# First layer: softmax in two halves, two score banks, output projection in four parts, POOL products in pieces of 512 elements

## What is computed

```python
x = x + tanh(g_xattn[0]) * xattn(layernorm(x), ctx, mask)   # 16 heads of 64, causal, then out @ Wo.T + bo
x = x + tanh(g_ffn[0])   * ffn(layernorm(x))
def ffn(x):
    h = rmsnorm(x) * gamma1
    q = h @ Wq + bq                                  # 16 heads of 16 per token
    k, v = split((h @ Wdown + bdown) @ Wup + bup)
    att = softmax(einsum('bthd,btgd->bthg', q, k) / 4)   # per token: 16 x 16 scores among its own heads
    x = x + einsum('bthg,btgd->bthd', att, v) @ Wo + bo
    h2 = rmsnorm(x) * gamma2
    gate = softmax(h2 @ Wg + bg)                     # 8 experts, all of them computed
    return x + sum_e gate_e * (h2 @ We_e)
```

## Time and profile before

| | |
|---|---|
| median of the runs | 2658.17 us |
| profiled execution, its own time / span | 2663.2 us / 2661.4 us |
| busy over the span | PE 87%, DVE 56%, ACT 48%, POOL 38% |
| granted TensorE clock over the span | 0.956 |
| one body of the loop in layer 0 | 78.4 us |

### The profile page before, as it was taken

One profiled execution on the slowest core, in us unless ns is written; L12 is line 12 of the kernel. 1 busy time (PEld: TensorE's weight loads), 2 busy tenths in 40 slices (PEclk: granted clock), 3 DMA queues, 4 the chain that ended last, 5 costly groups with the idle time before them and its releaser, 6 DMA issues. The chain is left out here.

```text
span 2661.4 us, 48220 instructions
## 1 busy us (share of the span) xinstructions
PE 2325.5 (87%) x16128; PEld 1931.7 (73%) x16128; DVE 1487.3 (56%) x3906; ACT 1268.0 (48%) x3971; POOL 1019.5 (38%) x910
## 2 busy tenths in 40 slices
PE   5888989888888898888466999999999999999998
PEld 4667777777777777776354777877777887777777
DVE  3467667666766676767635445444444544444441
ACT  5655566555556555556023444433344443334441
POOL 1355554555554455555512333222233322223320
PEclk9989999999999999999667999999999999999999
DMA  4000000000000000000040000000000000000000
GB/s 145 14 6 17 13 16 4 16 16 16 16 12 4 16 16 16 16 4 9 4 161 1 13 17 16 16 16 16 4 12 16 16 16 16 16 4 12 16 9 9
DMA packets 25856, 51.66 MB, mean 19 GB/s; under 512 B 6272, under 2 KB 7040, under 8 KB 24640
## 3 DMA queue, kind: packets, MB, share of 16 engines
q1 hardware_dynamic: 25792, 50.84, 5.7%
HBM read 42.44 MB, written 8.39 MB: 19 GB/s over the span
## 5 line engine op out<-in xcount | busy, mean ns | idle before, releaser
L1191 POOL TENSOR_SCALAR l_probs<-l_probs,l_rinv 128x256 f32<-128x256 f32 x512 | 238.4, 480 | 590.0 <-DVE l_rinv L1406 589.4
L1302 ACT ACTIVATE l_probs<-l_score,l_negmax 128x256 f32<-128x256 f32 x512 | 238.4, 472 | 265.0 <-DVE l_negmax L1401 265.0
L364 POOL TENSOR_TENSOR l_prod<-l_att,l_kv 128x2048 f32<-128x2048 f32 x64 | 287.4, 4527 | 180.7 <-DVE l_att L637 180.7
L350 POOL TENSOR_TENSOR l_prod<-l_q,l_kv 128x2048 f32<-128x2048 f32 x64 | 290.3, 4547 | 155.9 <-DVE l_att L620 84.1
L1606 PE MATMUL l_ffn<-l_w,l_hid 128*128 128x256 f32 x1536 | 347.9, 382 | 1.0 <-ACT l_hid L1276 1.0
L1606 PEld LDWEIGHTS l_ffn<-l_w,l_hid 128*128 128x128 f32 x1536 | 287.6, 190 | 51.0 <-issue 14.3
L1413 DVE COPY l_probsT<-l_attn 128x512 f32<-128x512 f32 x256 | 175.5, 685 | 161.1 <-PE l_attn L1569 160.9
L710 DVE CUSTOM_DVE_ANT_0 l_probs<-l_score,l_mbias 128x256 f32<-128x256 f32 (+1 forms) x512 | 161.3, 353 | 147.5 <-PE l_score L906 97.6
L1401 DVE TENSOR_REDUCE l_negmax<-l_score 128x2 f32<-128x512 f32 x256 | 175.1, 684 | 65.4 <-PE l_score L1557 65.4
L643 DVE TENSOR_REDUCE l_h<-l_prod 128x128 f32<-128x2048 f32 x64 | 146.3, 2286 | 110.7 <-POOL l_prod L364 110.7
L439 ACT ACTIVATE l_probs<-l_probs,l_negmax 128x256 f32<-128x256 f32 x256 | 130.8, 511 | 107.7 <-DVE l_negmax L710 106.5
(11 more groups left out here) (271 smaller groups left out, 7527.2 us busy)
## 6 DMA issues: line engine op xcount, KB each, us to landing
l_ctxin<-in_ctx SPq DMA_DIRECT2D x32, 256.0 KB, 3.0
l_xin<-in_x SPq DMA_DIRECT2D x16, 256.0 KB, 2.7
l_x<-in_x SPq DMA_DIRECT2D x16, 256.0 KB, 2.6
x<-l_acc SPq DMA_DIRECT2D x16, 256.0 KB, 2.0
l_xin<-x SPq DMA_DIRECT2D x16, 256.0 KB, 3.3
l_x<-x SPq DMA_DIRECT2D x16, 256.0 KB, 2.6
out<-l_x SPq DMA_DIRECT2D x16, 256.0 KB, 2.0
l_hid<-in_w SPq DMA_DIRECT2D x2, 1536.0 KB, 8.6
```

The source lines that it names most:

```text
L350: nc.gpsimd.tensor_tensor(prod[:, u].rearrange("p (h g d) -> p h g d", h=half, g=H), q4[:, u * half:(u + 1) * half].unsqueeze(2).to_broadc ...
L364: nc.gpsimd.tensor_tensor(prod[:, u].rearrange("p (h d g) -> p h d g", h=half, d=HD), a4.unsqueeze(2).to_broadcast([P, half, HD, H]), v4.u ...
L1191: last = nc.gpsimd.tensor_scalar(probs[:, j % 4, t * S:(t + 1) * S], probs[:, j % 4, t * S:(t + 1) * S], rinv[:, j, t:t + 1], 1.0, ALU.mul ...
L1302: last = nc.scalar.activation(probs[:, s % 4, t * S:(t + 1) * S], ps[:, t * S:(t + 1) * S], ACT.Exp, bias=negmax[:, s, t:t + 1], accum_out ...
```

## The change

What it does: `attn_out` takes two of eight chunks at a time, at steps 10, 14, 18 and after step 19, and adds them up in a bank of its own (`outer`); for that bank `score` goes from three to two. The mix steps move up and `down` comes before `q`. Scores, softmax and gather move up, the softmax is done per half of the tokens, and POOL's second products wait for their half alone. Each POOL product is written as four instructions of 512 elements per partition.

```diff
+PART = 2
-        attn = Banks(nc, ctx, "l0_attn", attn_uses + ["out"], ahead=["xT", "k0", "k1", "k2", "v0", "v2"])
-        mix_at = {2: "hT", 3: "q", 4: "down", 5: "up0", 6: "up1"}
+        outer = Banks(nc, ctx, "l0_outer", ["out"], 1)
+        attn = Banks(nc, ctx, "l0_attn", attn_uses + ["idle"], ahead=["xT", "k0", "k1", "k2", "v0", "v2"])
+        mix_at = {1: ("hT",), 2: ("down", "q"), 3: ("up0",), 4: ("up1",)}
-        score_at = {7: 0, 9: 1, 11: 2, 12: 3}
-        gather_at = {15: 0, 16: 1, 18: 2, 19: 3}
-        score = Banks(nc, ctx, "l0_score", [f"s{j}" for j in range(H)] + ["idle0", "idle1"], 3)
+        score_at = {6: 0, 7: 1, 9: 2, 10: 3}
+        soften_at, divide_at = {7: 0, 10: 1}, {8: 0, 11: 1}
+        gather_at = {11: 0, 13: 1, 14: 2, 16: 3}
+        score = Banks(nc, ctx, "l0_score", [f"s{j}" for j in range(H)])
         side = SideBanks(nc, ctx, "l0_side", mix_uses, moe_uses,
-                         ["oT", "out", "hT", "q", "down", "h2T", "up0", "gate", "up1"] + ...
+                         ["oT", "out", "hT", "down", "q", "up0", "up1", "h2T", "gate"] + ...
 query_key (POOL), and weigh (POOL) in the same way:
-                    nc.gpsimd.tensor_tensor(
-                        prod[:, u].rearrange("p (h g d) -> p h g d", h=half, g=H),
-                        q4[:, u * half:(u + 1) * half].unsqueeze(2).to_broadcast([P, half, H, HD]),
-                        k4.unsqueeze(1).to_broadcast([P, half, H, HD]), ALU.mult).then_inc(prod_ready, 1)
+                    for h in range(0, half, PART):
+                        last = nc.gpsimd.tensor_tensor(
+                            out[:, h:h + PART], q4[:, u * half + h:u * half + h + PART].unsqueeze(2).to_broadcast([P, PART, H, HD]),
+                            k4.unsqueeze(1).to_broadcast([P, PART, H, HD]), ALU.mult)
+                    last.then_inc(prod_ready, 1)
 weigh:
+                    if u == 0:
+                        pool.wait_ge(att_ready, 2 * b + t + 1)
                     if piece < 2:
-                        pool.wait_ge(att_ready, b + 1)
+                        pool.wait_ge(scored, 4 * b + piece + 3)
 beside_head (ACT), now after the projections' copies:
-                    if b is not None and s == 12:
-                        act.wait_ge(sub_ready, b + 1)
-                        nc.scalar.activation(att[:], att[:], ACT.Exp, scale=HD ** -0.5).then_inc(aexp_done, 1)
+                    if b is not None and s in soften_at:
+                        t = soften_at[s]
+                        act.wait_ge(sub_ready, 2 * b + t + 1)
+                        nc.scalar.activation(att[:, t], att[:, t], ACT.Exp, scale=HD ** -0.5).then_inc(aexp_done, 1)
 DVE: mix_softmax_max(b, t) and mix_softmax_divide(b, t) work on att[:, t]; a drain behind the divide is gone
+                        if s in soften_at:
+                            mix_softmax_max(b, soften_at[s])
+                        if s in divide_at:
+                            mix_softmax_divide(b, divide_at[s])
 PE:
+                def attn_out(a, j):
+                    ps, full, free, turn = outer.at("out", a)
+                    heads.emptied(pe, f"o{j}", a)
+                    if j == 0:
+                        ...
+                        pe.wait_ge(free, turn)
+                    for t in range(NT):
+                        for c in (2 * j, 2 * j + 1):
+                            last = T.matmul(ps[:, t * D:(t + 1) * D], oT[:, c, t * P:(t + 1) * P], wo[:, c, :],
+                                            start=t == 0 and c == 0, stop=t == NT - 1 and c == NC0 - 1)
+                    if j == 3:
+                        last.then_inc(full, 1)
+                            if s in (10, 14, 18):
+                                attn_out(a, (s - 10) // 4)
                     if a is not None:
-                        score.skip(pe, "idle0", a)
-                        score.skip(pe, "idle1", a)
+                        attn.skip(pe, "idle", a)
+                        attn_out(a, 3)
```

More of the change, by code:

```diff
@@ L363, in weigh @@
                     a4 = att[:, t].rearrange("p (h g) -> p h g", g=H)[:, u * half:(u + 1) * half]
-                    nc.gpsimd.tensor_tensor(prod[:, u].rearrange("p (h d g) -> p h d g", h=half, d=HD),
-                                            a4.unsqueeze(2).to_broadcast([P, half, HD, H]), v4.unsqueeze(1).to_broadcast([P, half, HD, H]),
-                                            ALU.mult).then_inc(prod_ready, 1)
+                    out = prod[:, u].rearrange("p (h d g) -> p h d g", h=half, d=HD)
+                    for h in range(0, half, PART):
+                        last = nc.gpsimd.tensor_tensor(out[:, h:h + PART], a4[:, h:h + PART].unsqueeze(2).to_broadcast([P, PART, HD, H]),
+                                                       v4.unsqueeze(1).to_broadcast([P, PART, HD, H]), ALU.mult)
+                    last.then_inc(prod_ready, 1)
                 def body(a, b, c, nxt):
@@ L470, in before_exp @@
                 def before_exp(b, c, s):
-                    if b is not None and mix_at.get(s) == "hT":
+                    if b is not None and "hT" in mix_at.get(s, ()):
                         high(side, "hT", b, hT[0], hT_hi, gamma1)
-                    if b is not None and mix_at.get(s) == "down":
+                    if b is not None and "down" in mix_at.get(s, ()):
                         ps, full, _, turn = side.at("down", b)
@@ L544, in _ @@
             def _(dve):
-                for banks in (attn, score, heads, side):
+                for banks in (attn, score, heads, outer, side):
                     banks.open(dve)
@@ L718, in attn_final @@
                 def attn_final(a):
-                    ps, full, free, turn = attn.at("out", a)
+                    ps, full, free, turn = outer.at("out", a)
                     dve.wait_ge(full, turn)
@@ L737, in beside_head @@
                             V.tensor_copy(x1res[:], x1[:]).then_inc(x1_copied, 1)
-                    if b is not None and s in mix_at:
-                        use = mix_at[s]
-                        if use == "hT":
-                            low(side, "hT", b, hT, hT_hi, gamma1)
-                        elif use == "q":
-                            mix_queries(b)
-                        elif use == "down":
-                            mix_down(b)
-                        else:
-                            mix_kv(b, int(use[2:]))
+                    if b is not None:
+                        for use in mix_at.get(s, ()):
+                            if use == "hT":
+                                low(side, "hT", b, hT, hT_hi, gamma1)
+                            elif use == "q":
+                                mix_queries(b)
+                            elif use == "down":
+                                mix_down(b)
+                            else:
+                                mix_kv(b, int(use[2:]))
                     if c is not None:
@@ L956, in beside_head @@
                 def beside_head(b, c, s):
-                    if b is not None and s in mix_at:
-                        use = mix_at[s]
-                        if use == "hT":
-                            pe.wait_ge(h_ready, b + 1)
-                            transpose4(side, "hT", b, h)
-                        elif use == "q":
-                            side.emptied(pe, "hT", b)
-                            tokens(side, "q", b, hT, fq, D)
-                        elif use == "down":
-                            mix_down(b)
-                        else:
-                            mix_up(b, int(use[2:]))
+                    if b is not None:
+                        for use in mix_at.get(s, ()):
+                            if use == "hT":
+                                pe.wait_ge(h_ready, b + 1)
+                                transpose4(side, "hT", b, h)
+                            elif use == "q":
+                                tokens(side, "q", b, hT, fq, D)
+                            elif use == "down":
+                                side.emptied(pe, "hT", b)
+                                mix_down(b)
+                            else:
+                                mix_up(b, int(use[2:]))
                     if c is not None:
```

46 lines of the change are left out of this document (18 added, 28 removed).

## The result

The changed kernel takes 2696.36 us (median, 2695.05 to 2697.15) against 2658.06 for the kernel before in the same session: ratio 1.0142 [1.0124 to 1.0159], 1.4% slower where 0.8% faster was forecast. Its profiled execution spans 2694.6 us at a mean granted clock of 0.946.

A forecast was written before the change was run, and what follows sets the result against it. PE was taken to set the pace, with some 13 us of waits and low clock per 78.4 us body. Terms 1.9 + 0 + 4.0 - 6.6 = -0.7 for 13 bodies (-9), edges -13.5, gave 2636 us, range 2602 to 2682.

The forecast's parts named there:

- step 6 to `attn_max` 7: Second part of a body, up to the end of attn_max 7 on DVE: 0 change, bounds 0 and +1 us.
- First term: Body start to the scores of step 6: +1.9 us from PE's waits for hT and h2T, bounds +0.5 and +3.
- Third term: attn_max 7 to the scores of step 12: +4.0 us from DVE's longer path, bounds +1 and +7.
- In the loop it is hidden: Extra time of POOL's shorter pieces, +2.4 us for eight products, claimed hidden in loop bodies as POOL starts 1.5 us earlier.
- my added 1.1 for the clock: Within attn_max 7 to step 12: a clock fall after the 2.4 us wait slows what leads to xT by 1.1 us.
- Fourth term: Scores of step 12 to the next start: -6.6 us as output work and waits go, bounds -4 and -7.5.
- POOL's pieces: POOL's products as four instructions of 512 elements each: +0.3 us per product, bounds 0 and +0.55.
- The edges: Draining body -4.5, body 15 -4, bodies 0 and 1 -2 and -3: together -13.5 us (-6 to -20).
- the two long bodies: Two profiled bodies of 81.5 and 80.9 us instead of 78.3, read as 5.8 us too much in the profiled execution.
- The slower rival: Clock falls at new waits before hT, at step 9, before step 12: 3.4 us per body, 2680 us; chance 0.30.

The follow-up runs named there:

- a_fill2: Changed kernel with dummy transposes in front of four PE waits, those of step 9 in the bank of the values' products; 2669.37 us, 1.0047.
- a_nopool: Changed kernel with POOL's products shrunk to 16 elements per instruction, waits, reduces and order as changed; 2651.95 us, 0.9973.
- b_fill: Kernel before with 20 dummy transposes ahead of the wait of 2.49 us for the low half of xT; 2650.94 us, 0.9966.
- b_quart: Kernel before with the output projection in four parts in its own bank and two score banks; 2659.5 us, 1.0007.
- b_2banks: Kernel before with two score banks instead of three, nothing else; 2657.48 us, 0.9991.
- v2: Kernel before with four-part output projection, two score banks, score reduces, whole softmax and gathers earlier, POOL's products whole; 2655.09 us, 0.9986.
- a_mixlate: Changed kernel with the mix steps back by one (hT at 2, down and q at 3, up0 at 4, up1 at 5); 2693.24 us, 1.0139.
- v3: Kernel before with only score reduces, softmax and gathers moved up one or two steps, three score banks; 2705.39 us, 1.0182.
- v2_nomax: v2 without the maximum and its subtraction in the per-token softmax, against the kernel before; 2669.94 us, 1.0046.
- a_p8: Changed kernel with POOL's products again as whole instructions of 2048 elements; 2836.03 us, 1.0653.

## Why the prediction was wrong

The prediction put a full body at 77.7 us, and it takes 81.9 on the mean. Two of its terms were too small: the first (+1.9, measured +3.7), which left out a fall of the clock, and the third (+4.0, measured +5.6), which took DVE's instructions at lengths that they have only when no POOL product runs beside them. A fall that comes in every second body was left out of the fourth.

By the prediction's own cuts, in the body from 408.20 (scores of step 6 at 437.19, end of `attn_max` 7 at 441.81, scores of step 12 at 464.78, next start 489.23); a_fill2 is the same schedule without low clock:

| part | predicted | measured | a_fill2 |
|---|---|---|---|
| start to step 6 | 27.2 (+1.9) | 29.0 (+3.7) | 27.5 |
| step 6 to `attn_max` 7 | 4.4 (0) | 4.6 (+0.2) | 4.6 |
| to the scores of step 12 | 21.4 (+4.0) | 23.0 (+5.6) | 23.0 |
| to the next start | 24.7 (-6.6) | 24.5 (-6.8); 26.2 in every second body | 24.5 |
| body | 77.7 | 81.0 and 82.8 | 79.5 |

*First term: the fall of the clock left out.* Its waits came as worked out (2.1, 0.4 and 1.6 predicted; 1.87, 0.46 and 1.51 measured). What I did not price is the clock behind 431: in a_fill2, with dummies in these waits, the part takes 27.5. The rival named falls behind hT, step 9 and step 12. One did come behind step 9, and one in every second body behind step 12; but the first came behind the gate product, where I had taken 1.51 us for harmless because it was so at the body's start.

*Third term: DVE's path taken too short.* I summed DVE's path with durations from places where POOL was still or doing something else. POOL's early start, which I counted as free ("In the loop it is hidden"), puts it beside just those instructions. In the stretch they take 1.02 us more for xn and 1.03 - 0.42, 1.47 - 0.42 and 1.03 - 0.42 for subtract, multiply, subtract: 3.3 us. My 20.3 of DVE's path and 3.3 are 23.6, measured 23.0. Without POOL's products (a_nopool) the stretch is 19.8, near my 20.3: the path was right but for the standing. The fall of the clock at 450 costs nothing: a_fill2 has none and needs the same 23.0, since PE spends there in waits what it gains. So here my added 1.1 for the clock was wrong too, and the term missed by 1.6 net. The trace of before had the sign of it, in a column that I did not read (min, median, max of one line):

```profile
L566 DVE TENSOR_SCALAR l_xn<-l_xin,l_mvA,l_rstdA x32: 394/410/3564, 15.0 to 1144.9; 128x256 f32<-128x256 f32 x32
```

The one of 3564 ns is in body 1. It runs from 121.15 to 124.71, and POOL's product beside it ends at 124.56, 0.15 us before. The loop had the sign too: of the 32 instructions of L671, 13, one in each full body, take 0.74 to 0.85 us, and end 0.15 us after a POOL instruction (L325):

```profile
115.58 8.98 POOL L350 TENSOR_TENSOR l_prod<-l_q,l_kv 128x2048 f32<-128x2048 f32 x2 [3.32 <-DVE l_kv L616]
...
L671 DVE TENSOR_SCALAR l_y<-l_y,l_r x32: 340/346/848, 179.7 to 1338.2; 128x256 f32<-128x256 f32 x32
```

*Fourth term: right*, -6.8 for -6.6, but for the third fall in every second body, 1.7 / 2 = 0.85 on the mean.

*POOL's pieces* were right in size (four take 4.96 to 5.32 us; forecast 4.8) and wrong in what they are for: they are not a small cost of the change but what it rests on. Whole products with these steps give 2836. But short ones alone, in the old order, cost 47 us (b_p2).

*The sum.* A mean body of 81.9 is 4.2 over the forecast: 1.8 first term, 0.2, 1.6 third, -0.2, 0.8 for the fall of every second body. 13 bodies at this mean are 55 us. The edges: from the profiles, body 0 ends 6.0 earlier (forecast 2) and all from the start of the first draining body on is 8.1 shorter (4.5), but bodies 1 and 15 are 0.3 and 4.5 longer instead of 3 and 4 shorter: -9.3 for -13.5. Together 59 of the 60 us between 2636 and 2696. One reading of the prediction was off without weight: by PE's starts the two long bodies of the kernel before take 81.4 and 79.8 us, 4.6 too much and not 5.8.

*The slower rival* gave 2680 with 3.4 us per body, from the clock alone. Clock falls do cost 2.4 per body (81.9 against 79.5). The other 2.7 between a_fill2 and the fall-free body of b_fill (25.3, 4.4, 16.6 and 30.6 us in the four parts, 76.8 in all) is a balance: 2.1 more at the start, 0.2, 6.5 more on DVE's path, 6.1 less at the end. Of the 6.5, 3.3 are DVE's standing. So not the clock but the path is the larger part of the difference, as before has 1.5 of clock in its 78.3 as well. Without the standing a fall-free body would be 79.5 - 3.3 = 76.2 by my estimate, 0.6 under the 76.8: even without the standing, little was to be gained. a_nopool, with falls, takes 78.4 to 80.8. The split takes the 74 dummies of a_fill2 as free, which no run tests.

Not settled: why a given set of waits makes one, two or three falls. Kernels with quite different waits lock at the same bodies (b_quart, b_2banks and mostly v2 at 78.3 to 78.5; a_mixlate and v3 at 81.9), and v2_nomax is slower than v2 though no wait of PE is over 0.6 us longer and one is 1.5 shorter.

## What to carry to other kernels

Before moving POOL work so that it runs beside DVE, list what DVE does in that time: here the operations with two inputs from SBUF, and TENSOR_SCALAR instructions with one, stood until POOL's current instruction ended, while reduces and operations with one input from PSUM did not. So put the latter there, or cut POOL's instructions short. Read min and max of a line, not only its mean: where they lie far apart for one shape, look whether the long ones end just after an instruction of POOL. And a wait added on TensorE is worth more or less than its length: waits of under 2 us close to each other had a fall of the clock behind them in most bodies here, while a fall ahead of a wait on DVE cost nothing.

## What the runs showed of the hardware

- DVE's 256-element subtraction of two SBUF inputs: 0.43 us without POOL's products (a_nopool), 1.03 in the median beside POOL instructions of 512 elements, 4.24 beside 2048 (a_p8); it ends 0.28 to 0.29 us after POOL's instruction, and a TENSOR_SCALAR of one SBUF input 0.15 after. Not stretched: reduces of one SBUF input, 2.26 to 2.29 us in all three kernels (before, changed, a_p8), and the experts' sums with one input from PSUM (L706), 456 to 484 ns in the changed kernel and 456 to 485 in a_p8.
- Elementwise products on POOL: 17.99 us for four of 2048 elements, 19.64 for sixteen of 512.
- The clock fell to 1.2 GHz behind waits of 0.47, 1.02, 0.40 and 0.28 us (b_fill), with PE busy in between, and did not in the next body with the same waits. In v2 a wait of 2.45 to 2.47 us before the scores of step 10 had a fall of the clock with it in two of twelve loop bodies and none in the others. One fall cost a body 1.5 us where PE is the bound (b_fill), 0 where DVE is (the changed kernel after 450).
- The list of waits doesn't order the kernels: v3 with waits up to 3.27 us and a_mixlate with 4.16 both take 81.9 us in most bodies.
